# A gated cross-attention block: the first chunk's attention by tiles of tokens, layer one begun on the first tile, and three weight steps moved

## The chip, the cores and the metric

The kernel runs on one core of a Trainium2 chip. The metric is the device time of one execution in microseconds (us). Times inside the trace are counted from the first instruction.

## The reference

```
x = x + tanh(g_xattn) * Attention(layernorm(x), ctx)       # 16 heads of 32, 128 keys per batch
x = x + tanh(g_ffn)   * FFN(layernorm(x))
Attention: Q = n @ Wq + bq; K, V = ctx @ Wk + bk, ctx @ Wv + bv
           softmax(Q K^T / sqrt(32)) V, then @ Wo + bo
FFN:       h = concat(n, -n); h = s0 * h @ (+-1 by k0); relu * 2      # 1024 -> 2048
           h = s1 * h @ (+-1 by k1); relu * 2; h = s2 * h @ (+-1 by k2)   # 2048 -> 2048 -> 512
```
x has 2 x 2048 tokens of 512 features, ctx 2 x 128 keys. All inputs are float32; k0, k1, k2 are booleans in 32-bit words.

## The kernel before

The 4096 tokens are taken in sixteen chunks of 256, each of two tiles of 128. Products are in float16 pairs (a high part and what it leaves, "hi" and "lo"); the weights of the FFN are signs in 8-bit floats, built on the chip from the words of k0, k1, k2. ScalarE makes the high parts, VectorE the low ones.

Every chunk's FFN is a list of 44 slots (`SLOTS`): eight of layer one (L0, one pair of output tiles each), two that end the chunk before, then layer one to two (L1) in four groups q of seven products, with the products of layer three (L2) between. Into these slots the attention of the next chunk is woven (`WEAVE`): in slots 10 to 24 the scores S of eight units, one slot later their probabilities (PS), from slot 15 the products with V (PV), from 28 the transposition and projection of the result (CT, WO), the second norm (N2, T2), and the first norm of the chunk after that (LN, N1, T1). A unit is four heads for one tile of tokens. All five engines walk the same lists in order; semaphores join them. Chunk 0 multiplies plainly; from chunk 1 on L1 uses seven products of half-size blocks instead of eight, for which VectorE makes sums of weights: `weight_step(q, step)`, at the slots of `LATE_WEIGHTS` (first table chunk 0, second chunk 1).

The attention of chunk 0 has nothing to be woven into. It is the opening, written out by hand as the list `FIRST`: LN, N1, T1 (transposition to xT), CQ (Wq split), CX (context transposed), SCALARS, then Q (query product of one group of four heads), QP and QD (its high and low part), K, KP (key product, scaled and split), KM (the key block masked by head), V, VP, and rounds k = 0 to 9 with S, EX (exponents), PT (transposition of the probabilities, split by ScalarE and then VectorE), PV (product with V, then on VectorE reciprocal, scaling and sum into attn), with extra items of `EARLY` and `MIDDLE` in each round. CO and CL split Wo, BO and XB add the output bias to x, W0 makes the signs of layer one (one item: four of its sixteen tiles). The slots of chunk 0 follow.

A bank is one of eight in PSUM. `FIRST_BANK` gives each item of the opening a bank, and TensorE waits in `begin` for the item that had it before.

The lines of the profile: L1043 transpositions, L1066 K, L1075 V, L1103 S, L1120 to L1122 Q, L1129 and L1130 PV, L1136 to L1138 WO, L1219 and L1220 layer one, L1252 and L1253 L1. On VectorE L942 is CQ, L912 CX, L919 KP, L801 the maxima, L756 the reciprocal that begins PV, L748 PT, L763 the sum into attn, L984 to L994 the weight steps; on ScalarE L526 is EX, L570 PT, L619 a copy of a partial sum.

Of the kernel before, what the change touches and what calls it, by code (L numbers as in the profile page):

```python
# [5 lines left out]
P = 128  # L6


def gated_block_kernel(nc: bass.Bass, x, ctx, g_xattn, g_ffn, Wq, Wk, Wv, Wo, bq, bk, bv, bo,
# [118 lines left out]
    for k in range(U + 2):  # L128
# [30 lines left out]
    with es:  # L159
# [82 lines left out]
        head_zero, head_made, k_masked, k_masked_0 = (sem(n) for n in ("head_zero", "head_made", "k_masked", "k_masked_0"))  # L242
# [30 lines left out]
        CUT = {"T1": 0, "CT": TT, "T2": 2 * TT}  # L273

# [139 lines left out]
        def _(pool):  # L414
# [10 lines left out]
            def prepare(item):  # L425
# [6 lines left out]
                if kind == "KM" and n:  # L432
                    pool.wait_ge(head_made, 4)
                    pool.wait_ge(k_lo, n + 1)
                    for hl in range(2):
                        pool.tensor_tensor(
                            Kb[:, hl, n, :].rearrange("p (j k) -> p j k", j=4),
                            KHL[:, hl, n, 0:P].rearrange("p (o k) -> p o k", o=1).to_broadcast([P, 4, P]),
                            own_head[:, :].rearrange("p (j o) -> p j o", o=1).to_broadcast([P, 4, P]),
                            ALU.mult).then_inc(k_masked, 1)  # L440
# [45 lines left out]
        def _(act):  # L486
# [44 lines left out]
            def query_parts(n, a, bank):  # L531
# [9 lines left out]
                if a == 0 and n >= 2:  # L541
                    act.wait_ge(s_done, nth(0, NU, TT * (n - 2) + TT - 1))
# [785 lines left out]
```

## Time and profile before

| | |
|---|---|
| median of 3 runs | 1574.0 us (1572.46 to 1574.11) |
| the profiled execution | 1570.58 us, span 1568.8 us |
| TensorE busy | 1523.2 us, 97% |
| VectorE busy | 938.5 us, 60% |
| ScalarE busy | 672.3 us, 43% |
| granted TensorE clock, mean | 0.996 |

Busy shares are means over the whole span. TensorE bounds the chunks, the opening is a chain over several engines.

### The profile page before, as it was taken

How to read it: one execution, taken by the hardware profiler on the slowest of the kernel's cores; microseconds unless marked ns; L12 is line 12 of the kernel's file. 1: busy time of each engine (PE TensorE's matmuls, PEld its weight loads, DVE VectorE, ACT ScalarE, POOL GpSimd, SP SyncE). 2: the span in 40 equal slices, each digit the busy share in tenths (PEclk: the TensorE clock that was granted, in tenths of full speed). 3: DMA queues.
4: the chain of work that ended last, by engine and by line, in shares of the span. 5: the costliest groups of instructions: out<-in, count | busy, mean ns of one | idle time of the engine just before them, and what ended most of it. 6: DMA issues, size and time to landing. Idle time of an engine off the chain costs nothing.

```text
span 1568.8 us, 46139 instructions
## 1 busy us (share of the span) xinstructions
PE 1523.2 (97%) x19872; PEld 1300.0 (83%) x19872; DVE 938.5 (60%) x1938; ACT 672.3 (43%) x1568; POOL 169.1 (11%) x273
## 2 busy tenths in 40 slices
PE   6798999999999999999999999999999999999998
PEld 4586888888988888898988888888898888889887
DVE  5877775656556565655656566465655656565441
ACT  3442342534535254452635445253553525345231
POOL 2202001020100202001020100101010010101000
PEclk9999999999999999999999999999999999999999
DMA  8443133242424334253442524333242432314100
GB/s 255 121 103 60 42 95 69 79 79 57 87 59 99 62 81 83 52 98 56 95 69 62 95 50 102 63 88 69 62 89 52 102 66 82 82 47 98 28 29 15
DMA packets 278227, 120.96 MB, mean 77 GB/s; under 512 B 243464, under 2 KB 259848, under 8 KB 277896
## 3 DMA queue, kind: packets, MB, share of 16 engines
q1 hardware_dynamic: 275960, 117.48, 34.6%
q8 instruction: 157, 2.57, 0.7%
q10 hardware_dynamic: 2064, 0.53, 0.2%
q14 instruction: 46, 0.38, 0.1%
HBM read 37.76 MB, written 16.78 MB: 35 GB/s over the span
## 4 chain that ended last, share of the span: by engine, by line
PE 87%; DVE 6%; ACT 3%; DMA 2%; issue 2%; SPq 0%; POOL 0%; DVEq 0%; ACTq 0%; POOLq 0%
PE bank L1252 22%; PE bank L1253 22%; PE bank L1219 7%; PE bank L1220 7%; PE bank L1269 6%; PE bank L1270 6%; PE bank L1136 2%; PE bank L1137 2%; PE bank L1138 2%; PE bank L1120 2%; PE bank L1121 2%; PE bank L1122 2%; ACT Pf L526 1%; PE bank L1164 1%; DMA PT<-Phl 1%
## 5 line engine op out<-in xcount | busy, mean ns | idle before, releaser
L1252 PE MATMUL bank<-H,W 128*128 128x128 f16 x6720 | 778.3, 219 | 8.3 <-ACT C L619 6.7
L1253 PE MATMUL bank<-H,W 128*128 128x128 f16 x6720 | 778.0, 219 | 0.0
L1252 PEld LDWEIGHTS bank<-H,W 128*128 128x128 fp8e5 x6720 | 655.3, 98 | 20.8 <-ACT C L619 12.3
L1253 PEld LDWEIGHTS bank<-H,W 128*128 128x128 fp8e5 x6720 | 657.4, 98 | 7.1
L1219 PE MATMUL bank<-hT,W 128*128 128x256 f16 x1024 | 226.8, 273 | 3.5 <-DVE hT L742 1.9
L1220 PE MATMUL bank<-hT,W 128*128 128x256 f16 x1024 | 226.8, 272 | 0.0
L526 ACT ACTIVATE Pf<-bank,nmax 128x128 f32<-128x128 f32 x512 | 145.9, 368 | 139.1 <-DVE nmax L801 137.4
L1269 PE MATMUL bank<-W,h 128*128 128x512 fp8e5 x512 | 194.0, 379 | 1.6 <-DVE h L849 1.6
L1270 PE MATMUL bank<-W,h 128*128 128x512 fp8e5 x512 | 194.0, 379 | 0.0
L473 POOL TENSOR_TENSOR attn<-pvs 128x128 f32<-128x128 f32 x120 | 75.6, 630 | 1002.8 <-DVE pvs L814 1002.8
L841 DVE TENSOR_TENSOR C<-bank,C 128x256 f32<-128x256 f32 x180 | 76.2, 423 | 161.8 <-ACT C L619 89.9
L619 ACT ACTIVATE C<-bank 128x256 f32<-128x256 f32 x180 | 69.7, 387 | 212.8 <-PE bank L1253 212.8
L805 DVE SCALAR_TENSOR_TENSOR Phl<-Pf,Phl 128x512 f16<-128x512 f32 x120 | 82.5, 688 | 91.7 <-ACT Phl L604 91.6
L836 DVE TENSOR_TENSOR H<-Fp,H 128x896 f16<-128x896 f32 (+1 forms) x128 | 135.2, 1058 | 0.8 <-ACT H L610 0.8
L644 ACT ACTIVATE Fp<-bank 128x512 f32<-128x512 f32 x128 | 76.4, 597 | 90.2 <-PE bank L1220 88.9
L615 ACT ACTIVATE H<-Fp 128x896 f16<-128x896 f32 x120 | 113.3, 944 | 1.8 <-DVE Fp L872 1.7
L849 DVE SCALAR_TENSOR_TENSOR h<-C,h 128x256 f16<-128x256 f32 x180 | 76.4, 424 | 61.2 <-ACT h L682 29.6
L1219 PEld LDWEIGHTS bank<-hT,W 128*128 128x128 fp8e5 x1024 | 100.2, 98 | 15.4 <-issue 4.0
L1220 PEld LDWEIGHTS bank<-hT,W 128*128 128x128 fp8e5 x1024 | 100.2, 98 | 11.4
L801 DVE TENSOR_REDUCE nmax<-bank 128x4 f32<-128x512 f32 x128 | 87.5, 683 | 17.7 <-PE bank L1164 16.6
L1269 PEld LDWEIGHTS bank<-W,h 128*128 128x128 f16 x512 | 50.0, 98 | 53.1 <-issue 1.7
L1270 PEld LDWEIGHTS bank<-W,h 128*128 128x128 f16 x512 | 50.0, 98 | 51.3
(129 smaller groups left out, 1911.3 us busy)
## 6 DMA issues: line engine op xcount, KB each, us to landing
Qst<-q_bounce SPq DMA_DIRECT2D x120, 128.0 KB, 2.8
Y<-in_x_dram SPq DMA_DIRECT2D x16, 512.0 KB, 3.8
R<-X SPq DMA_DIRECT2D x16, 512.0 KB, 3.5
q_bounce<-Qhl SPq DMA_DIRECT2D x120, 64.0 KB
out_dram<-R SPq DMA_DIRECT2D x15, 512.0 KB, 2.7
W<-in_L_ffn_k_dram SPq DMA_DIRECT2D x8, 512.0 KB, 8.2
W<-in_L_ffn_k_dram SPq DMA_DIRECT2D x2, 1024.0 KB, 18.7
PT<-Phl SPq DMA_TRANSPOSE x120, 3.1
```

Of the source, the lines that this page charges most:

```text
L526: last = nc.scalar.activation(Pf[:, n % 2, j * P:(j + 1) * P], bank[:, j * P:(j + 1) * P], ACT.Exp, bias=nmax[:, n % 2, j:j + 1], scale=1.0)
L615: nc.scalar.activation(H0[:, 0, i], Fp[:, i % 3, 1:8, :], ACT.Copy).then_inc(l0_hi, 1)
L644: nc.scalar.activation(Fp[:, n % 3, 0:4, :], banks[n % 3][:, :].rearrange("p (b n) -> p b n", b=4), ACT.Relu)\
L801: V_.tensor_reduce(nmax[:, n % 2, :], bank[:, :].rearrange("p (j k) -> p j k", j=4), AX.X, ALU.max, negate=True).then_inc(s_max, 1)
L805: V_.scalar_tensor_tensor(out=Phl[:, n % 2, 1, :], in0=Pf[:, n % 2, :], scalar=PS, in1=Phl[:, n % 2, 0, :], op0=ALU.mult, op1=ALU.subtract)\
L836: V_.tensor_tensor(H0[:, 1, i, rows, :], Fp[:, i % 3, of, :], H0[:, 0, i, rows, :], ALU.subtract)\
L1219: mm(o, w, hT[:, k, :], start=k == 0, stop=False)
L1220: last = mm(o, w, hT[:, KT + k, :], start=False, stop=k == KT - 1)
L1252: mm(o, w, H0[:, 0, i, b_of, :], start=first, stop=False, skip_group_check=True)
L1253: last = mm(o, w, H0[:, 1, i, b_of, :], start=False, stop=i == PAIRS - 1, skip_group_check=True)
L1269: mm(banks[3 + t][:, :], hi, w2, start=q == 0 and h == 0 and jj == 0, stop=False)
L1270: last = mm(banks[3 + t][:, :], lo, w2, start=False, stop=q == GROUPS - 1 and h == 1 and jj == 1)
```

## The change

In the opening:
- A unit n of chunk 0 is now group n % 4 of tile n // 4 (`unit`), so the first tile goes through all heads first. Queries and keys of all four groups are made by round 1; groups 2 and 3 of the queries get a home of their own in Qst.
- CT for the first tile comes in round 5, WO0 in round 7, N2 and W0's first item in round 8, T2 in round 9. After the second tile's CT the first tile of pairs 0, 1 and 2 of layer one is computed (`L0T`, `layer_one(n, 0, P)`); the slots of chunk 0 then compute only the second tile of these pairs.
- `WARM`: 14 products of zeros before T1 and 6 before the scalars, into bank 1, which nobody reads.
- The context's transpositions use banks 4 and 5 instead of 6 and 7; the transposed context moves from hT to H0; keys' float copies share four places.
- The low mask of the keys moves from POOL to VectorE for groups 1 to 3; the high one stays.
- The second item of W0 moves from slot 0 of chunk 0 into the opening.

In chunk 1: the weight steps (3, 2), (3, 3), (3, 4) move from slots 15, 19, 23 to 25, 29, 33.

```diff
-    FIRST = first(("LN", 0), ("LN", 1), ("N1", 0), ("N1", 1), ("T1", 0), ("T1", 1), ("CQ", 0), ("CQ", 1), ("CQ", 2),
-                  ("CQ", 3), ("CX", 0), ("CX", 1), ("SCALARS", 0), ("Q", 0), ("Q", 1), ("QP", 0), ("QD", 0),
-                  ("K", 0), ("KP", 0), ("QP", 1), ("KM", 0), ("K", 1), ("KP", 1), ("KM", 1), ("QD", 1), ("S", 0))
-    EARLY = {1: first(("KP", 2), ("KM", 2)), 2: first(("QP", 2), ("VP", 0)), 3: first(("KP", 3), ("KM", 3)),
-             4: first(("QP", 3)), 5: first(("KP", 4)), 6: first(("KP", 5)), 7: first(("KP", 6)), 8: first(("KP", 7))}
-    MIDDLE = {0: first(("V", 0), ("K", 2)), 1: first(("V", 1), ("Q", 2)), 2: first(("QD", 2), ("K", 3)),
-              3: first(("Q", 3), ("BO", 0)), 4: first(("QD", 3), ("XB", 0), ("K", 4), ("CO", 0)),
-              5: first(("XB", 1), ("K", 5), ("CL", 0), ("CO", 1)), 6: first(("K", 6), ("CL", 1), ("CO", 2)),
-              7: first(("K", 7), ("CL", 2), ("CO", 3)), 8: first(("CL", 3)), 9: first(("W0", 0))}
+    FIRST = first(("LN", 0), ("LN", 1), ("N1", 0), ("N1", 1), ("WARM", 14), ("T1", 0), ("T1", 1), ("CQ", 0), ("CQ", 1),
+                  ("CQ", 2), ("CQ", 3), ("CX", 0), ("CX", 1), ("WARM", 6), ("SCALARS", 0), ("Q", 0), ("Q", 1),
+                  ("QP", 0), ("QD", 0), ("K", 0), ("KP", 0), ("QP", 1), ("KM", 0), ("K", 1), ("KP", 1), ("KM", 1),
+                  ("QD", 1), ("Q", 2), ("K", 2), ("S", 0))
+    EARLY = {0: first(("QP", 2), ("KP", 2), ("KM", 2), ("QD", 2)),
+             1: first(("QP", 3), ("KP", 3), ("KM", 3), ("QD", 3)), 2: first(("VP", 0)),
+             5: first(("KP", 4)), 6: first(("KP", 5)), 7: first(("KP", 6)), 8: first(("KP", 7))}
+    MIDDLE = {0: first(("Q", 3), ("K", 3), ("V", 0)), 1: first(("V", 1), ("CO", 0)), 2: first(("CO", 1), ("CL", 0)),
+              3: first(("CO", 2), ("CL", 1), ("BO", 0)), 4: first(("K", 4), ("CO", 3), ("CL", 2), ("XB", 0)),
+              5: first(("K", 5), ("CL", 3), ("XB", 1)), 6: first(("K", 6)), 7: first(("K", 7), ("WO", 0)),
+              8: first(("N2", 0), ("W0", 0)), 9: first(("T2", 0))}
...
-        FIRST += first(("CT", k - 8)) if k >= 8 else []
-    FIRST += [(1, ("LN", 0)), (1, ("LN", 1))]
-    FIRST += first(("WO", 0), ("WO", 1), ("N2", 0), ("N2", 1), ("V", 2), ("V", 3), ("T2", 0), ("T2", 1))
+        FIRST += first(("CT", 0)) if k == 5 else []
+    FIRST += first(("CT", 1), ("W0", 1), ("V", 2), ("WO", 1), ("L0T", 0), ("L0T", 1), ("V", 3)) + [(1, ("LN", 0))]
+    FIRST += first(("N2", 1)) + [(1, ("LN", 1))] + first(("T2", 1), ("L0T", 2))
...
-    FIRST_FFN = {0: ("W0", 1), 1: ("W0", 2), 3: ("W0", 3), 5: ("VP", 1)}
+    FIRST_FFN = {1: ("W0", 2), 3: ("W0", 3), 5: ("VP", 1)}
...
-                    {11: (2, 4), 15: (3, 2), 19: (3, 3), 23: (3, 4)})
+                    {11: (2, 4), 25: (3, 2), 29: (3, 3), 33: (3, 4)})
+    def unit(n, a):
+
+        return divmod(n, TT) if a else (n % G, n // G)
...
-    KIND_BANKS = {"V": (4, 4), "S": (0, 1), "PT": (2, 3), "PV": (4, 5), "T1": (2, 3), "CT": (2, 3), "WO": (0, 1)}
+    KIND_BANKS = {"CX": (4, 5), "V": (4, 4), "S": (0, 1), "PT": (2, 3), "PV": (4, 5), "T1": (2, 3), "CT": (2, 3), "WO": (0, 7)}
...
+                if kind == "WARM":
+                    pe.wait_ge(zeros_made, 1)
+                    idle = PT[:, 1].rearrange("p a n -> p (a n)")
+                    for _ in range(n):
+                        mm(banks[1][:, :], idle[:, 0:P], idle[:, 0:4 * P], start=True, stop=True)
...
+                if kind == "L0T":
+                    pe.wait_ge(w0_made, n + 2)
+                    pe.wait_ge(first_lo, FIRST_CUT["T2", 0])
+                    layer_one(n, 0, P)
...
+            def layer_one(n, begin, end):
+
+                for half in range(2):
+                    o = banks[n % 3][:, half * CHUNK + begin:half * CHUNK + end]
+                    tile = n + half * PAIRS
+                    for k in range(KT):
+                        w = W0[:, k, tile * P:(tile + 1) * P]
+                        mm(o, w, hT[:, k, begin:end], start=k == 0, stop=False)
+                        last = mm(o, w, hT[:, KT + k, begin:end], start=False, stop=k == KT - 1)
+                return last
...
+                    begun = f == 0 and ("L0T", n) in FIRST_BANK
+                    layer_one(n, P if begun else 0, CHUNK).then_inc(l0_done, 1)
```

## Rows read from the trace of the kernel before

**Rows 1.** The page, busy us by engine (share of the span, instructions).
```profile
PE 1523.2 (97%) x19872; PEld 1300.0 (83%) x19872; DVE 938.5 (60%) x1938; ACT 672.3 (43%) x1568; POOL 169.1 (11%) x273
```
**Rows 2.** Timeline of TensorE, layer one's first product in chunks 0 to 3.
```profile
74.01 0.27 PE L1219 MATMUL bank<-hT,W 128*128 128x256 f16 x1 [1.88 <-DVE hT L742]
...
177.75 0.27 PE L1219 MATMUL bank<-hT,W 128*128 128x256 f16 x1 [1.63 <-DVE h L856]
...
274.07 0.27 PE L1219 MATMUL bank<-hT,W 128*128 128x256 f16 x1
...
366.77 0.27 PE L1219 MATMUL bank<-hT,W 128*128 128x256 f16 x1
```
**Rows 3.** Waits of TensorE in 0 to 74 us: us in total, times, longest.
```profile
PE bank L1129 <- DVE PT L748: 5.8, 6, 1.5
```
**Rows 4.** Timeline of ScalarE and VectorE late in the opening's rounds.
```profile
53.02 1.12 ACT L526 ACTIVATE Pf<-bank,nmax 128x128 f32<-128x128 f32 x4
...
55.17 0.69 DVE L748 SCALAR_TENSOR_TENSOR PT<-bank,PT 128x512 f16<-128x512 f32 x1 [0.51 <-ACT PT L570]
...
59.47 0.17 DVE L756 RECIPROCAL rden<-bank 128x4 f32<-128x4 f32 x1
```
**Rows 5.** Windows: length, busy PE, PEld, DVE, ACT, POOL, granted clock, DMA share, GB/s.
```profile
15.70:19.10 3.40, 3.40 (x18) 2.36 (x17) 1.93 (x12) 1.00 (x3) 0.00 (x0) 0.50 1.05 407
...
60.00:63.40 3.40, 2.83 (x9) 1.61 (x10) 3.23 (x10) 0.60 (x1) 0.00 (x0) 0.51 0.30 79
```
**Rows 6.** Timeline of TensorE in chunk 1, the two waits in question.
```profile
221.64 0.23 PE L1252 MATMUL bank<-H,W 128*128 128x128 f16 x1 [2.34 <-ACT C L619]
...
236.47 0.22 PE L1252 MATMUL bank<-H,W 128*128 128x128 f16 x1 [0.61 <-DVE h L849]
```
**Rows 7.** Timeline of VectorE ahead of the first of them.
```profile
214.87 2.28 DVE L986 SCALAR_TENSOR_TENSOR W<-W 128x2048 fp8e5<-128x2048 fp8e5 x1
```
**Rows 8.** The chain in the opening: start, us on it; two scores, eight products.
```profile
23.04 1.75 PE bank L1103 x8
```
**Rows 9.** Timeline of the opening's first steps, all engines, and of one late step.
```profile
8.55 1.97 PE L1043 MATMUL bank<-ident,xn 128*128 128x128 f32 x8 [8.55 <-DVE xn L783]
...
11.80 2.48 DVE L942 SCALAR_TENSOR_TENSOR Wq_lo<-W,Wq_hi 128x512 f16<-128x512 f32 x4
...
14.94 0.28 PE L1120 MATMUL bank<-xT,Wq_hi 128*128 128x256 f16 x1 [2.71 <-DVE hT L912]
...
15.65 0.20 ACT L517 ACTIVATE c<-scal 128x2 f32<-128x2 f32 x1 [2.42 <-DMA scal<-in_L_ffn_s_dram]
...
20.40 0.35 DVE L919 TENSOR_SCALAR Qst<-bank,bk_c 128x128 f32<-128x128 f32 x1 [2.01 <-PE bank L1066]
...
71.10 1.04 PE L1043 MATMUL bank<-ident,xn 128*128 128x128 f32 x8
```
**Rows 10.** Timeline, POOL beside VectorE; L763 min/median/max ns; POOL's masks as a group.
```profile
46.52 1.27 POOL L443 TENSOR_TENSOR X<-Y,bo_b 128x512 f32<-128x512 f32 x1
...
46.90 1.04 DVE L763 TENSOR_TENSOR attn<-pvs 128x128 f32<-128x128 f32 x1
...
L763 DVE TENSOR_TENSOR attn<-pvs x8: 291/292/1045, 37.2 to 60.1; 128x128 f32<-128x128 f32 x8
...
L436 POOL TENSOR_TENSOR h<-Fp,own_head 128x512 f16<-128x512 f16 x6 | 6.2, 1047 | 0.4
```
**Rows 11.** Windows of VectorE alone: WO's work, then one W0 item.
```profile
65.26:67.02 1.76, 1.62 (x3) 1.00 0.19 58
78.47:80.71 2.24, 2.10 (x7) 1.00 0.61 115
```
**Rows 12.** Timeline of TensorE: the second product of 256 columns, and two of 128.
```profile
74.12 0.27 PE L1220 MATMUL bank<-hT,W 128*128 128x256 f16 x1
...
1540.95 0.22 PE L1252 MATMUL bank<-H,W 128*128 128x128 f16 x1
1541.00 0.22 PE L1253 MATMUL bank<-H,W 128*128 128x128 f16 x1
```

More of the change, by code:

```diff
@@ L273, in gated_block_kernel @@
         CUT = {"T1": 0, "CT": TT, "T2": 2 * TT}
+        FIRST_CUT = {item: n + 1 for n, item in enumerate(i for i in FIRST_ITEMS if i[0] in CUT)}
         def nth(chunk, per_chunk, n):
@@ L284, in gated_block_kernel, with query_home @@
             c[:, n:n + 1] for n in range(13))
+        def query_home(n, a):
+            return Qhl_later[:, n - 2] if a == 0 and n >= 2 else Qhl[:, n % 2]
         def wait_apart(engine, semaphore, value):
@@ L289, in wait_apart, with mask_keys @@
             engine.nop(nofuse=True)
+        def mask_keys(engine, n, hl, semaphore):
+            engine.tensor_tensor(
+                Kb[:, hl, n, :].rearrange("p (j k) -> p j k", j=4),
+                KHL[:, hl, n, 0:P].rearrange("p (o k) -> p o k", o=1).to_broadcast([P, 4, P]),
+                own_head[:, :].rearrange("p (j o) -> p j o", o=1).to_broadcast([P, 4, P]),
+                ALU.mult).then_inc(semaphore, 1)
         block = es.enter_context(nc.Block())
@@ L433, in prepare @@
                     pool.wait_ge(head_made, 4)
[L434 to L440, printed above, removed]
+                    mask_keys(pool, n, 0, k_masked_hi)
             def add_bias(a, t):
@@ L469, in attend @@
                 if kind == "PV" and a:
-                    g, t = divmod(n, TT)
+                    g, t = unit(n, a)
                     pool.wait_ge(pv_scaled, nth(a, NU, n))
@@ L540, in query_parts @@
                     act.wait_ge(s_done, nth(0, NU, TT * (n + 2) + TT - 1))
-                if a == 0 and n >= 2:
-                    act.wait_ge(s_done, nth(0, NU, TT * (n - 2) + TT - 1))
-                nc.scalar.activation(Qhl[:, n % 2, 0, :], bank[:, 0:CHUNK], ACT.Identity,
+                nc.scalar.activation(query_home(n, a)[:, 0, :], bank[:, 0:CHUNK], ACT.Identity,
                                      bias=bq_c[:, n:n + 1], scale=1 / (XS * WS))
@@ L553, in attend_first @@
                 if kind in CUT:
-                    act.wait_ge(first_turned, CUT[kind] + n + 1)
+                    act.wait_ge(first_turned, FIRST_CUT[item])
                     if kind == "CT":
@@ L751, in attend_first @@
                 if kind == "PV":
-                    g, t = divmod(n, TT)
+                    g, t = unit(n, 0)
                     v = bank.rearrange("p (j n) -> p j n", j=4)
@@ L930, in prepare @@
                         .then_inc(v_lo, 1)
-                if kind == "KM" and n == 0:
+                if kind == "KM":
                     dve.wait_ge(head_made, 4)
-                    for hl in range(2):
-                        dve.wait_ge(k_lo if hl else k_hi, 1)
-                        V_.tensor_tensor(
-                            Kb[:, hl, 0, :].rearrange("p (j k) -> p j k", j=4),
-                            KHL[:, hl, 0, 0:P].rearrange("p (o k) -> p o k", o=1).to_broadcast([P, 4, P]),
-                            own_head[:, :].rearrange("p (j o) -> p j o", o=1).to_broadcast([P, 4, P]),
-                            ALU.mult).then_inc(k_masked_0, 1)
+                    if n == 0:
+                        dve.wait_ge(k_hi, 1)
+                        mask_keys(V_, 0, 0, k_masked)
+                    dve.wait_ge(k_lo, n + 1)
+                    mask_keys(V_, n, 1, k_masked)
                 if kind == "CQ":
@@ L1001, in last_weights @@
                     .then_inc(w2_made, 1)
+            V_.memset(PT[:, 1], 0.0).then_inc(zeros_made, 1)
             V_.memset(own_head[:, :], 0.0).then_inc(head_zero, 1)
@@ L1092, in begin @@
                         pe.wait_ge(wq_lo, KT)
[L1093 removed]
+                        pe.wait_ge(first_lo, FIRST_CUT["T1", TT - 1])
                     queries(n, bank)
                 if kind == "S":
[L1096 removed]
+                    g, t = unit(n, 0)
                     pe.wait_ge(q_lo, g + 1)
[L1098 to L1101 removed]
+                    pe.wait_ge(k_masked, g + 2)
+                    if g > 0:
+                        pe.wait_ge(k_masked_hi, g)
                     for i, (hl_q, hl_k) in enumerate(((0, 0), (1, 0), (0, 1), (1, 1))):
[L1103 removed]
+                        last = mm(bank[:, :], query_home(g, 0)[:, hl_q, t * P:(t + 1) * P], Kb[:, hl_k, g, :],
                                   start=i == 0, stop=i == 3)
@@ L1123, in queries, with weighted @@
                 last.then_inc(q_done, 1)
-            def weighted(n, bank, batch):
-                g, t = divmod(n, TT)
+            def weighted(n, bank, a):
+                batch = a // PER_BATCH
+                g, t = unit(n, a)
                 for j in range(4):
@@ L1157, in attend @@
                 if kind == "S":
-                    g, t = divmod(n, TT)
+                    g, t = unit(n, a)
                     if n == 0 and a == 1:
@@ L1168, in attend @@
                     pe.wait_ge(p_crossed[n % 2], nth_sent(a, NU, n))
-                    weighted(n, bank, batch)
+                    weighted(n, bank, a)
                 if kind == "WO":
@@ L1213, in feed @@
                         pe.wait_ge(l1_sum, nth(f - 2, NC, NC - 1))
-                    for half in range(2):
-                        o = banks[n % 3][:, half * CHUNK:(half + 1) * CHUNK]
-                        for k in range(KT):
-                            tile = n + half * PAIRS
-                            w = W0[:, k, tile * P:(tile + 1) * P]
-                            mm(o, w, hT[:, k, :], start=k == 0, stop=False)
-                            last = mm(o, w, hT[:, KT + k, :], start=False, stop=k == KT - 1)
-                    last.then_inc(l0_done, 1)
+                    begun = f == 0 and ("L0T", n) in FIRST_BANK
+                    layer_one(n, P if begun else 0, CHUNK).then_inc(l0_done, 1)
                 if kind == "L1" and f == 0:
```

29 lines of the change are left out of this document (13 added, 16 removed).

## Prediction

> **What bounds the kernel now.** I read the page first: TensorE is busy 97% of the span and VectorE 60% [rows 1]. So the time is the opening before TensorE's work becomes dense, then sixteen chunks of dense products, and what is gained in between is what TensorE waits for less. The timeline of TensorE gives the frame: layer one of chunk 0 begins at 74.01, of chunk 1 at 177.75, of chunk 2 at 274.07, of chunk 3 at 366.77 [rows 2]. The third chunk took 92.70 us, the second 96.32 for the same products, 3.6 more.
>
> The timeline of the opening shows 8.6 us before the first transposition (x and its norm must come) and 2.7 before the first product for the queries [rows 9], the view of waits 5.8 in six waits for VectorE's half of the transposed probabilities (PT) [rows 3]. The opening has two parts. To some 35 us it is a line of dependent steps (queries, keys, first scores). From there to the end VectorE and ScalarE set the pace: in the last full round ScalarE's exponents start at 53.02, VectorE's PT only at 55.17, after 0.51 of waiting for ScalarE's [rows 4], and TensorE waits for the latter. Three stretches of 3.4 us ran at a granted clock of 0.50 or 0.51, that is 1.2 GHz, in the midst of it (the first and the last in [rows 5]).
>
> **The change, part by part.** It has two halves that do not touch: the new order of the opening, and three weight steps moved in chunk 1. I work each out against the profiled execution (span 1568.8, run 1570.6) and carry the difference to the median, 1574.0, which is 3.4 above that run.
>
> *Weight steps.* Steps 2, 3 and 4 for group 3 go from slots 15, 19 and 23 of chunk 1 to 25, 29 and 33. In chunk 1 TensorE waited 2.34 us at 221.64 and 0.61 at 236.47 [rows 6], 2.95 together. The first is on ScalarE's copy of a partial sum (L619), which in its order stands behind exponents, and those wait for VectorE's maxima; VectorE was late with them because the step at L986 held it for 2.28 us from 214.87 [rows 7]. Slots 15 to 24 are also those where VectorE does the maxima and the low halves for eight units. From slot 25 on no maxima are left. Slot 25 has one low half, slots 29 and 30 the end of a unit. The last step ends in slot 33 and is needed at slot 35: TensorE has slot 34's products and an output projection between. I cost the new places at nothing; if the step of slot 33 delays the second norm instead, there are ten slots to the next chunk. Bounds: 3.6 us if all that chunk 1 has over chunk 2 goes, nothing if the waits come back in the later slots. I take 2.95.
>
> *Warm products.* Fourteen zero products of 512 columns before T1 wait only for a memset; two scores' eight took 1.75 at the full clock [rows 8], so 14 take 3.1 us, 6.1 at half of it, and both end before T1's start at 8.55 [rows 9]. They cost nothing. What they can give is T1: eight transpositions took 1.97 there and 1.04 at 71.10. T1 is on the path to VectorE's split of Wq, which starts at 11.80 [rows 9] behind T1's low halves; I take 0.7 earlier. Against it: Wq must have landed, and 2.48 us of splitting follow anyway. The six before the queries fill a hole in which TensorE waits for that split.
> The Trainium skill ("TensorE: Matmul & The Clock Gate", Part 1) says that the array's default is the throttled clock and sustained activity releases it, which would favour the warm products; its Part 4 says that transpositions do not count as activity. By the last, T1 itself stays slow and the sum is 0.7 worse; the trace shows only that later transpositions are fast.
>
> *Context on banks 4 and 5.* The first query product waited until 14.94 for VectorE's copy of the context out of bank 6 [rows 9]. Now it waits for the split alone, another 0.6. With the 0.7 it starts at 13.6, and at 2.4 GHz both query groups take 2.6 us, where 4.3 were spent because of the first low stretch. But the next step, ScalarE's take of the queries, sits behind the scalars, and their tanh starts at 15.65 because of a transfer [rows 9]. So the first key comes to VectorE at 18.0 instead of 20.40: 2.4 gained.
>
> *Q2 and K2 ahead of S0, Q3 and K3 ahead of S2.* Those are the same products, done earlier. S0 comes to 22.6, against 23.0 now [rows 8]. From K1 to the first transposed probabilities TensorE then has 12.5 us of work (S at 0.87 [rows 8], Q 12 products at 0.11 [rows 2, 12]; K 0.9 and V 1.75 in the same chain) in one row, to 32.1.
>
> *The masks of heads 1 to 3.* POOL keeps the high one (1.05 us each), VectorE takes the low one. Both read SBUF and both are released by the same event, so they start together. Whether they collide the trace tells: VectorE's sum of two SBUF tensors takes 0.29, but 1.04 when POOL's bias add was under way from 46.52, and it then ended just as that did [rows 10]. So each low mask waits one POOL mask, 1.05, three times. Two of these lie beside TensorE's row of work; I leave 0.7 on the path. Bounds 0 and 3.1.
> The Trainium skill ("SBUF — State Buffer", Who interferes with whom) says that a VectorE instruction with two SBUF inputs and a GpSimd one that reads SBUF share a port, and the one that starts second blocks fully. The trace agrees in the row just named; it speaks against this part of the change.
>
> *The rounds.* I then laid the new order out engine by engine with the durations above. The eighth exponents start at 53.6, against 53.02 [rows 4]. Nothing is won by then: the rounds are lighter by the early keys and queries, but V's split now stands ahead of the third exponents, and CT0 stands before the seventh, costing 1.1.
> Behind it is the costly part. Output projection WO0 is now between PV5 and PT6 on TensorE and on VectorE. After PV5 comes K7 (0.9), then WO0 (12 products of 512 columns, as scores have them, at 1.75 / 8 [rows 8], 2.6). VectorE has nothing in that time and idles 2.6 us, then works on WO0 for 1.76 [rows 11]; then W0's first item, 2.24 [rows 11], stands ahead of the last PT. So the last PV reaches VectorE at 65.1, 5.6 later than the 59.47 of before [rows 4]. What remains is shorter by that much: WO1 alone, 68.4 to 71.0; VectorE and POOL's norm to 73.9; T21 at 74.5; its halves of hT to 76.5. Layer one of chunk 0 starts at 76.6 instead of 74.01.
> But by then three pairs have their first tile done. A product of 256 columns is issued each 0.11 us [rows 2, 12], one of 128 each 0.055 [rows 12], so the split costs nothing, and each of the three pairs has 0.88 left of 1.75. Pair 3 starts at 76.6 + 2.64 = 79.24; before it was 74.01 + 5.25 = 79.26. The opening comes out even. Bounds: 2.6 sooner with the masks uncollided and a wait less in the rounds; 5 later, below.
>
> *The rest.* The second W0 item leaves slot 0 of chunk 0; the third must be made by pair 4 at 81.0 and ends at 80.5 to 81: no wait, none to spare. On SP's queue the bounce of the keys waits for the last key, 3 to 4 us later than before; its landing is needed by layer one at 76.6 and the stacked keys by 95. Other SP items (second x, W2, k1) wait on the same events at about the same times. Nothing there.
>
> Sum: 0.0 for the opening, −2.95 for chunk 1: 1574.0 − 2.95 = 1571.0 (0.19% less).
>
> **The rivals.** A change within 0.2%, 3.1 us, can't be told from none here.
> - *Even opening, weight waits gone.* The forecast, 1571.0, own range 1569.4 to 1572.7. Chance 0.45. It sits on the bound of what can be told, so half of it counts as faster.
> - *The opening gains too.* For: three low stretches cost it some 5 us of TensorE time before (three times 3.4 at half [rows 5]), the denser row of work from 19 to 32 has none of the pauses; if the masks do not collide (0.7) and the rounds keep 2 more of the 2.4 gained at 18 us, the opening gives 3 and the time is 1568. Against: two thirds of that is beside ScalarE's and VectorE's chain. Chance 0.27.
> - *Slower: WO0 amid the rounds at 1.2 GHz.* From 43 to 65 us TensorE is now sparser than before, and the stretch at 60.00 [rows 5] shows that the clock falls there even now. WO0 is 2.6 us more at half clock, with VectorE waiting behind it; V2 and WO1 1.8 and 2.6 more. With both, the opening is 5 to 7 later and the time 1576 to 1578; it decides once more than 2.95 is lost, that is WO0 and a good part of another. Against: before, only half a projection fell into it. Chance 0.13.
> - *The weight steps only move their wait.* At slots 29 and 33 a 2.28 us step ahead of the unit's end or of the norm makes the transposes late; then 1574, no change. Against: TensorE's slot is 3.5 us and the step starts at its beginning. Chance 0.15.
>
> **How the numbers follow.** Faster by over 0.2%: 0.27, and 0.20 of the first: 0.47. Within: 0.25 of the first and 0.14 of the last: 0.39. Slower: 0.13 and 0.01: 0.14. The range takes in the second and the last and the near end of the third: 1566.5 to 1575.5.
>
> **What would show it.** In the trace after: chunk 1 at 93.0 to 93.7 us instead of 96.3; first query product near 13.6; first key on VectorE near 18; low masks of 1.8 us beside POOL; an idle 2.6 us on VectorE before WO0's add; layer one at 76 to 77, and the fourth pair near 79.2. A fourth pair by 76.5, or after 82, would make the prediction wrong, as would a wait of over 1 us in slots 25 to 35 of chunk 1. The granted clock between 50 and 70 us decides between the second and the third.

## The result, and the profile after

The changed kernel took 1578.0 us, the one before 1572.5 on the same chip (medians of 11 runs each). The ratio is 1.0037, with a 95% interval of 1.0028 to 1.0045: 5.8 us slower by the ratio (the medians differ by 5.5), where 3.0 faster had been forecast, and outside the range of 1566.5 to 1575.5. The 1574.0 that the forecast started from was the median of the first three executions of the kernel before. One of the eleven executions of the changed kernel took 5630 us; nothing here explains it, and it is left out of the ratio. The profiled execution took 1578.46, span 1576.7, which is 7.9 more than the span of before. That is 2 more than the ratio says, since the traced execution of before was a short one (1570.58, against a median of 1572.5).

The page of the changed kernel, busy time by engine. Against [rows 1] TensorE is busy 6.5 us more, with 68 more products: 20 are the products of zeros and 48 come from the split of three pairs. VectorE has 4.4 more, and POOL 4.2 less. How much of this lies on the path the page cannot say; the timeline can:

```profile
PE 1529.7 (97%) x19940; PEld 1302.1 (83%) x19940; DVE 942.9 (60%) x1942; ACT 672.8 (43%) x1568; POOL 164.9 (10%) x270
```

The timeline of TensorE after, layer one's products: the first of `L0T`, the first second-tile one (slot 0), the fourth pair, the fifth, then chunks 1, 2 and 3. Columns are start, duration, operands, and in brackets the idle time before with what ended it:

```profile
77.54 0.22 PE L1147 MATMUL bank<-hT,W 128*128 128x128 f16 x1
83.42 0.22 PE L1147 MATMUL bank<-hT,W 128*128 128x128 f16 x1 [0.76 <-DVE hT L756]
86.10 0.27 PE L1147 MATMUL bank<-hT,W 128*128 128x256 f16 x1
89.31 0.28 PE L1147 MATMUL bank<-hT,W 128*128 128x256 f16 x1 [1.31 <-DVE W L983]
187.12 0.27 PE L1147 MATMUL bank<-hT,W 128*128 128x256 f16 x1 [1.63 <-DVE h L870]
281.62 0.27 PE L1147 MATMUL bank<-hT,W 128*128 128x256 f16 x1
374.28 0.27 PE L1147 MATMUL bank<-hT,W 128*128 128x256 f16 x1
```

Read against [rows 2], this is where the time went. The fourth pair starts at 86.10; before it started at 74.01 + 5.25 = 79.26. That is 6.8 later. The fifth waits 1.31 for its signs and is 8.3 late (it started at 81.00 before). The rest of chunk 0 costs another 1.1 (187.12 against 177.75 is 9.4); in it TensorE waits 1.38 for xT, which it did not before, and 1.24 instead of 0.59 for the stacked queries. Chunk 1 then took 94.50 instead of 96.32 and gave 1.8 back; from chunk 2 on nothing moves (92.66 here, 92.70 before).

So the loss is in the opening. Its steps after, from the timelines of ScalarE, VectorE and POOL; they answer to [rows 4, 9, 10]:

```profile
16.59 0.20 ACT L533 ACTIVATE c<-scal 128x2 f32<-128x2 f32 x1 [4.14 <-DMA scal<-in_L_ffn_s_dram]
18.85 0.35 DVE L935 TENSOR_SCALAR Qst<-bank,bk_c 128x128 f32<-128x128 f32 x1
23.59 1.04 POOL L307 TENSOR_TENSOR h<-Fp,own_head 128x512 f16<-128x512 f16 x1
23.73 1.44 DVE L307 TENSOR_TENSOR h<-Fp,own_head 128x512 f16<-128x512 f16 x1 [0.95 <-POOL Fp L452]
56.62 1.12 ACT L542 ACTIVATE Pf<-bank,nmax 128x128 f32<-128x128 f32 x4
61.95 0.75 DVE L835 SCALAR_TENSOR_TENSOR X<-bank,c,X 128x512 f32<-128x512 f32 x1 [4.28 <-PE bank L1173]
69.94 0.18 DVE L770 RECIPROCAL rden<-bank 128x4 f32<-128x4 f32 x1 [0.78 <-PE bank L1165]
```

The eighth exponents start at 56.62 where the forecast had 53.6: 3.0 late. VectorE then idles 4.28 before WO0's add where it had 2.6: 1.7 more. The last PV reaches VectorE at 69.94, forecast 65.1: 4.8 late. Second-tile layer one starts at 83.42, forecast 76.6: 6.8 late.

The windows of the changed kernel show where TensorE was slow. Columns: stretch, length, busy time and count of PE, PEld, DVE, ACT, POOL, then the granted clock, DMA share, GB/s:

```profile
20.30:23.70 3.40, 3.38 (x17) 2.97 (x18) 1.25 (x3) 0.31 (x1) 0.49 (x2) 0.55 1.05 386
43.30:46.70 3.40, 3.40 (x22) 2.90 (x23) 1.92 (x5) 0.50 (x1) 0.57 (x1) 0.57 0.00 0
57.40:60.80 3.40, 3.40 (x11) 1.28 (x10) 0.27 (x1) 0.35 (x2) 0.00 (x0) 0.51 0.90 197
69.30:72.70 3.40, 3.15 (x18) 2.69 (x19) 1.65 (x4) 1.21 (x2) 0.00 (x0) 0.50 0.29 85
```

In four stretches the mean granted clock is 0.50 to 0.57, that is, TensorE ran at 1.2 GHz for all or nearly all of them: K1 and the start of Q2; K4, a transposition and scores; the first two thirds of WO0 (VectorE is busy 0.27 of 3.40); the transpositions of the second tile's result and V2. Of V2 the timeline says it plainly; at the full clock, in experiment 2, it took 1.89:

```profile
71.93 3.18 PE L1095 MATMUL bank<-W,H 128*128 128x256 f32 x8
```

### The profile page after: what moved, and what is told of

The parts are those of the page before. It is cut to its first block, busy times and chain, and to the rows that moved or that the text cites. A ratio compares the mean times of both kernels' runs of the same rounds, so it can differ in the third digit from the quotient of the medians.

```text
span 1576.7 us, 46288 instructions
## 1 busy us (share of the span) xinstructions
PE 1529.7 (97%) x19940; PEld 1302.1 (83%) x19940; DVE 942.9 (60%) x1942; ACT 672.8 (43%) x1568; POOL 164.9 (10%) x270
## 4 chain that ended last, share of the span: by engine, by line
PE 85%; DVE 7%; ACT 4%; issue 2%; DMA 2%; ACTq 0%; POOL 0%; SPq 0%; DVEq 0%; POOLq 0%
PE bank L1281 21%; PE bank L1282 21%; PE bank L1298 7%; PE bank L1299 7%; PE bank L1147 7%; PE bank L1148 7%; PE bank L1171 2%; PE bank L1172 2%; PE bank L1173 2%; ACT Pf L542 2%; PE bank L1154 2%; PE bank L1155 2%; PE bank L1156 2%; PE bank L1199 1%; DVE nmax L815 1%
## 5 line engine op out<-in xcount | busy, mean ns | idle before, releaser
L1281 PEld LDWEIGHTS bank<-H,W 128*128 128x128 fp8e5 x6720 | 655.3, 98 | 17.9 <-ACT C L633 10.1
L1147 PE MATMUL bank<-hT,W 128*128 128x256 f16 (+1 forms) x1048 | 227.2, 270 | 3.7 <-DVE h L870 1.6
L1148 PE MATMUL bank<-hT,W 128*128 128x256 f16 (+1 forms) x1048 | 227.3, 270 | 0.0
L1147 PEld LDWEIGHTS bank<-hT,W 128*128 128x128 fp8e5 x1048 | 102.5, 98 | 15.6 <-issue 2.8
L1148 PEld LDWEIGHTS bank<-hT,W 128*128 128x128 fp8e5 x1048 | 102.6, 98 | 11.3
```

The source lines that it names most:

```text
L1147: mm(o, w, hT[:, k, begin:end], start=k == 0, stop=False)
L1148: last = mm(o, w, hT[:, KT + k, begin:end], start=False, stop=k == KT - 1)
L1281: mm(o, w, H0[:, 0, i, b_of, :], start=first, stop=False, skip_group_check=True)
```

## The experiments

Theory A, after reading the trace: the loss is the clock, which falls in the sparser rounds, with WO0's two engines in line behind each other. Theory B: the new order itself costs the time (VectorE idle in WO0, W0 ahead of the last PT, masks beside POOL), at any clock. Ratios are to the kernel before, timed beside each run.

Where traces are compared one caution holds. Kernels with the same code in the opening did not have the same opening in time: layer one began at 74.01 in the trace of before and at 75.75 in that of e1, at 71.75 in that of e6 and at 70.19 in that of e12. So a single time in the opening is good to some 1.7 us, and a smaller difference between two traces shows nothing by itself.

**1. The parts alone, in the old order.** Only the table of weight steps (e1); only the warm products (14, and 6 ahead of the scalars) and the context's banks (e2); both (e5).

```diff
# e1_weights_only
-                    {11: (2, 4), 15: (3, 2), 19: (3, 3), 23: (3, 4)})
+                    {11: (2, 4), 25: (3, 2), 29: (3, 3), 33: (3, 4)})
# e2_early_only
-    FIRST = first(("LN", 0), ("LN", 1), ("N1", 0), ("N1", 1), ("T1", 0), ("T1", 1), ("CQ", 0), ("CQ", 1), ("CQ", 2),
+    FIRST = first(("LN", 0), ("LN", 1), ("N1", 0), ("N1", 1), ("WARM", 14), ("T1", 0), ("T1", 1), ("CQ", 0), ("CQ", 1), ("CQ", 2),
...
-    KIND_BANKS = {"V": (4, 4), "S": (0, 1), "PT": (2, 3), "PV": (4, 5), "T1": (2, 3), "CT": (2, 3), "WO": (0, 1)}
+    KIND_BANKS = {"CX": (4, 5), "V": (4, 4), "S": (0, 1), "PT": (2, 3), "PV": (4, 5), "T1": (2, 3), "CT": (2, 3), "WO": (0, 1)}
```

> The kernel before with only the three weight steps moved. Theory (the two halves are independent, the opening alone made the change slow): the opening is as before, chunk 1 takes 94.5 us instead of 96.3 as it did in the changed kernel, and the time is 1.8 to 2.9 us less than before. Rival (the weight steps' new slots cost something further on, in chunk 1 or 2): the time is as before or above it, and a new wait for a transposed probability or for the norm is seen at slots 29 to 35.

> The kernel before with only the products of zeros (14 and 6) and the context on banks 4 and 5. Theory (the early part is sound and its gain is lost later): first query product at 13.7, first key on VectorE 1.5 to 2.4 us sooner than 20.40, and some of that, 0.5 to 1.5 us, reaches layer one; the time is 0 to 1.5 us less than before. Rival (the early part itself costs, by moving the low-clock stretch from the queries to a costlier place): layer one begins later than 74.0.

> The kernel before with the early part (14 and 6 unused products, context on banks 4 and 5) and the moved weight steps, without the new order. Theory (the two gains are in different places and add): ratio near 0.9984 times 0.9989, 0.9973, 4 us less than before. Rival (the early gain was noise of the clock's phase): 0.9984 as with the weights alone.

Measured: weights alone 0.9984 (0.9975 to 0.9992), 2.5 us; early part alone 0.9989 (0.9980 to 0.9998), 1.7 us; both 0.9973 (0.9963 to 0.9983), 4.2 us. The two add up. Layer one of chunk 0 started at 72.40 with the early part (before 74.01); this 1.6 alone would be within the spread of traces, the ratio is what shows the gain.

With the weight steps alone chunk 1 took 94.01 instead of 96.32, and these waits of TensorE are left in it (columns: total, times, longest):

```profile
PE bank L1219 <- DVE h L856: 1.6, 1, 1.6
PE bank L1252 <- ACT C L619: 0.6, 1, 0.6
PE bank L1129 <- DMA PT<-Phl: 0.5, 1, 0.5
```

The 2.34 of [rows 6] is gone. The last line is for the transposed probabilities. In the changed kernel it is 0.99, and VectorE's timeline shows the step of slot 25 ahead of the low half of the last unit:

```profile
244.16 2.28 DVE L1000 SCALAR_TENSOR_TENSOR W<-W 128x2048 fp8e5<-128x2048 fp8e5 x1
246.91 0.68 DVE L819 SCALAR_TENSOR_TENSOR Phl<-Pf,Phl 128x512 f16<-128x512 f32 x1
```

The table is not the whole cause of that wait, since e2, which has the old table, shows 0.8 of it, and before shows none.

What follows: the changed kernel is these two parts and the new order (with the masks and `L0T` in it). 1.0037 / 0.9973 is 1.0064, so the new order costs some 10 us, nearly twice the loss that the ratio shows. By the two intervals together the 10 is good to about 2.

**2. The clock held.** The changed kernel with 45 more products of 512 columns, in places where TensorE waited; they write to banks that nobody reads at the time. Nothing of the order changes.

```diff
+    HOLD = {0: (4, 1, 0), 1: (6, 1, 0), 2: (8, 7, 4), 3: (6, 7, 6), 4: (7, 6, 7), 5: (14, 6, 7)}
+    for n, kind, m in ((0, "K", 0), (1, "K", 1), (2, "PV", 2), (3, "PV", 5), (4, "PV", 6), (5, "PV", 7)):
+        FIRST.insert(FIRST.index((0, (kind, m))), (0, ("HOLD", n)))
...
+                if kind == "HOLD":
+                    count, to, keys = HOLD[n]
+                    if keys:
+                        pe.wait_ge(k_float, keys)
+                    for _ in range(count):
+                        mm(banks[to][:, :], Wq_hi[:, 0, 0:P], Wq_hi[:, 0, 0:4 * P], start=True, stop=True)
```

> The changed kernel with 45 more unused products of 512 columns in six holes of TensorE: before K0, K1, PV2, PV5, PV6 and PV7. They read the high part of Wq and write banks that are free there. Theory A (the opening is slow because the clock falls to 1.2 GHz in K1, in round 4, in WO0 and in T2, V2): these stretches vanish, WO0 takes 2.6 us instead of 4.3 and V2 1.9 instead of 3.2, the fourth pair of layer one starts 4 to 6 us earlier, the time is 4 to 6 us less than the changed kernel's, at or below that of before. Rival B (the order makes it slow: WO0 and W0 stand ahead of the last PT on VectorE): at most 1.5 us of it comes back.

Measured: 1.0010 (1.0001 to 1.0019), so 0.9973 of the changed kernel, 4.2 us less, with the two intervals apart. The same four windows of this kernel:

```profile
20.30:23.70 3.40, 3.40 (x31) 2.87 (x29) 2.13 (x4) 0.78 (x2) 1.42 (x2) 1.00 1.07 391
43.30:46.70 3.40, 2.76 (x26) 1.90 (x23) 2.87 (x7) 1.94 (x6) 1.21 (x2) 1.00 0.02 5
57.40:60.80 3.40, 2.82 (x25) 1.74 (x24) 2.73 (x7) 0.91 (x2) 0.95 (x3) 1.00 0.61 118
69.30:72.70 3.40, 3.40 (x36) 2.33 (x35) 2.54 (x6) 0.00 (x0) 0.00 (x0) 1.00 0.35 95
```

And its timeline at five of the forecast's steps, with V2 among them:

```profile
53.92 1.12 ACT L545 ACTIVATE Pf<-bank,nmax 128x128 f32<-128x128 f32 x4
57.57 0.75 DVE L838 SCALAR_TENSOR_TENSOR X<-bank,c,X 128x512 f32<-128x512 f32 x1 [2.60 <-PE bank L1182]
65.36 0.18 DVE L773 RECIPROCAL rden<-bank 128x4 f32<-128x4 f32 x1 [0.59 <-PE bank L1174]
66.93 1.89 PE L1104 MATMUL bank<-W,H 128*128 128x256 f32 x8
79.80 0.27 PE L1156 MATMUL bank<-hT,W 128*128 128x256 f16 x1
83.02 0.28 PE L1156 MATMUL bank<-hT,W 128*128 128x256 f16 x1 [1.30 <-DVE W L986]
```

Forecast were 53.6, an idle 2.6, 65.1 and 79.24. With the clock at its full level the schedule worked out holds to 0.6 us; of the 6.8 that the fourth pair was late, 6.3 went. So theory A holds for the opening. Not all of the 6.3 is the clock: in this trace the scalars' transfer also came 0.9 sooner, which brought the first key forward by 0.5 (18.36 against 18.85). And the trace is of this kernel's shortest execution (1571.39, median 1573.11), so what the clock costs in time is better read from the ratio, 4.2. But the time stays 0.1% above before, not below it, so B holds too, for the rest: the fifth pair's wait of 1.30 does not depend on the clock, and see 4.

**3. WO0 later.** The changed kernel with W0's first item and WO0 behind the last PT instead of between PV5 and PT6.

```diff
-              5: first(("K", 5), ("CL", 3), ("XB", 1)), 6: first(("K", 6)), 7: first(("K", 7), ("WO", 0)),
-              8: first(("N2", 0), ("W0", 0)), 9: first(("T2", 0))}
+              5: first(("K", 5), ("CL", 3), ("XB", 1)), 6: first(("K", 6)), 7: first(("K", 7))}
+    at = FIRST.index((0, ("PV", 7)))
+    FIRST[at:at + 1] = first(("W0", 0), ("WO", 0), ("PV", 7), ("N2", 0), ("T2", 0))
```

> The changed kernel with WO0, N2 and the first W0 item behind the last PT (order PT7, W0, WO0, PV7, N2, T2) and nothing else. Theory A (clock): WO0 is still at 1.2 GHz or the next stretch is; 0 to 2 us come back. Rival B (order): VectorE no longer idles for WO0 and the last PT does not wait for 2.24 us of W0, so the last PV reaches VectorE 3 to 4 us sooner and 3 to 5 us come back.

Measured: 1.0025 (1.0015 to 1.0035), 1.9 us less than the changed kernel, but the intervals overlap. That is what theory A expected (0 to 2) and less than B's 3 to 5. The fourth pair starts at 85.15 instead of 86.10, in the trace of the longest of nine executions. WO0 now ran at the full clock (its products take 0.38 each), but TensorE stood at 0.50 to 0.54 from 40.0 to 50.2, and again over V2 and the start of WO1:

```profile
85.15 0.27 PE L1148 MATMUL bank<-hT,W 128*128 128x256 f16 x1
71.70:75.10 3.40, 3.40 (x11) 1.87 (x11) 2.83 (x8) 0.00 (x0) 0.00 (x0) 0.60 0.52 128
```

**4. The order, with the clock held in both.** The old order with 27 products that hold the clock (e6), on top of the two parts of experiment 1; and the new order with experiments 2 and 3 together (e7).

```diff
# e6_early_weights_hold: e5 and, by the same "HOLD" item (the first of them waits for q_split)
+    HOLD = {0: (5, 7, 3), 1: (3, 6, 5), 2: (5, 7, 6), 3: (5, 6, 7), 4: (2, 6, 7), 5: (2, 6, 7), 6: (5, 6, 7)}
+    for n, kind, m in ((0, "PV", 0), (1, "PV", 4), (2, "PV", 5), (3, "PV", 6), (4, "CT", 0), (5, "PV", 7), (6, "CT", 1)):
# e7_hold_later: e3 and e4, with
+    HOLD = {0: (4, 1, 0), 1: (6, 1, 0), 2: (8, 7, 4), 3: (6, 7, 6), 4: (6, 6, 7), 5: (12, 6, 7)}
```

> The kernel before with the early part, the moved weight steps and 27 more unused products in seven holes of the old order (before PV0, PV4 to PV7, CT0, CT1). Theory (the two stretches at 1.2 GHz that the old order has left, at some 36 and 60 us, cost it 2 to 3 us): another 1 to 3 us less than with the early part and weights alone, layer one 1 to 3 us sooner, no window of the opening below a clock of 0.9. Rival (those stretches lie beside VectorE's and ScalarE's chain): no difference.

> The changed kernel with the unused products in its holes and also WO0, N2 and the first W0 item behind the last PT. Theory (with the clock held, what is left of the loss is the order: VectorE idle for WO0 and the last PT behind W0): 2 to 3 us less than with the holes filled alone, so 1 to 3 us less than before. Rival (the order is innocent, as the same move brought little without the held clock): within 1 us of the kernel with filled holes alone.

Measured: e6 0.9961 (0.9948 to 0.9975), median 1566.45 of five executions; e7 0.9996 (0.9988 to 1.0005).

e7 is e4 with such products added and nothing else, so it is experiment 2 over again: from 1.0025 to 0.9996, 4.5 us less, with the intervals apart. So two pairs of kernels show the clock's price in the new order. Against e3, e7 is 2.2 us less, as the theory said (2 to 3), but the intervals overlap and its trace does not have the fourth pair sooner (80.13 against 79.80): that WO0's place costs 2 us is likely and not shown.

Between 58 and 61.5 us, the windows of e5 (first) and e6 (second) differ in the clock:

```profile
58.00:61.50 3.50, 3.50 (x11) 1.79 (x12) 3.36 (x9) 0.60 (x1) 0.00 (x0) 0.50 0.28 79
```
```profile
58.00:61.50 3.50, 3.18 (x24) 1.64 (x24) 3.27 (x10) 0.60 (x1) 0.00 (x0) 1.00 0.81 178
```

yet VectorE is as busy in the one as in the other (3.36, 3.27). In the old order VectorE sets the pace there, so a slow TensorE should cost little. e6 against e5 is 0.9988, 1.9 us, good to about 2.6: that fits, but it shuts out neither nothing nor a price as in the other. In the new order one of the slow stretches lies where VectorE waits (0.27 busy), and the clock is worth 4.2 and 4.5.

The order still loses 0.0035 between e6 and e7, some 5.5 us. The fourth pair comes at 80.13 in e7, and at 71.75 + 5.25 = 77.00 in e6, which is 3.1 of it, and the fifth pair's wait is another 1.3. The remaining 1 us wasn't traced.

```profile
80.13 0.27 PE L1157 MATMUL bank<-hT,W 128*128 128x256 f16 x1
```
```profile
71.75 0.27 PE L1235 MATMUL bank<-hT,W 128*128 128x256 f16 x1 [1.88 <-DVE hT L746]
```

One stretch of e7 (37.5 to 41, granted 0.54) and of e6 (20.5 to 23.9, 0.60) stayed slow. The pair e3 and e9 (see 8) has no slow stretch in the opening on either side, and shows the same: e9's fourth pair is at 69.91 + 5.25 = 75.16, 4.6 ahead of e3's, and its ratio 0.9968 against 1.0010 is 6.6 us less. The four traces of the new order with such products have the fourth pair at 78.56 to 80.67 (e8, e3, e7, e10), the three of the old order at 75.16 to 77.00 (e9, e12, e6).

**5. The third W0 item sooner.** e7 with W0's item in slot 0 instead of slot 1 of chunk 0.

```diff
-    FIRST_FFN = {1: ("W0", 2), 3: ("W0", 3), 5: ("VP", 1)}
+    FIRST_FFN = {0: ("W0", 2), 3: ("W0", 3), 5: ("VP", 1)}
```

> As the previous one, with the third W0 item at slot 0 of chunk 0 instead of slot 1, ahead of the first norm. Theory (the fourth pair's successor waits 1.3 us for that item because the norm and T1 stand ahead of it): that wait goes, and if the norm's transfer to xT is not late for the queries in slot 4, the time is 0.5 to 1.3 us less than the previous one's. Rival (the queries then wait for the transfer instead): no difference, with a wait of about 1 us at the first query product.

Measured: 1.0012 (1.0003 to 1.0021), 2.5 us more than e7, with the intervals just touching: no gain, and probably a loss. TensorE's waits from 78 to 180 have no line for W0 any more, and these two ahead of the rest:

```profile
PE bank L1174 <- DMA PT<-Phl: 3.4, 2, 2.7
PE bank L1164 <- DMA xT<-xs: 2.5, 1, 2.5
```

In e7 the first line is the same 3.4, the second is the 1.3 for W0, and there is none for xT. L1164 is the first query product, where the rival put the new wait, but at 1 us. So the wait moved to another place and grew; which of VectorE's steps passed it on wasn't traced.

**6. The masks.** e3 with both masks of groups 1 to 3 on POOL.

> The changed kernel with its holes filled, and both masks of groups 1 to 3 on POOL again. Theory (each low mask on VectorE takes 1.44 us beside POOL's against 0.78 alone, so the split brings little): within 1 us of the kernel with filled holes, either way; the first probabilities' split starts within 0.7 us of 32.8. Rival (the masks on two engines are what lets the scores come early): 1.5 to 3 us more.

Measured: 1.0001 (0.9992 to 1.0010) against e3's 1.0010; the split of the first probabilities starts at 32.71, as expected (32.8). POOL's two masks in a row:

```profile
22.50 2.04 POOL L310 TENSOR_TENSOR h<-Fp,own_head 128x512 f16<-128x512 f16 x2
```

In the changed kernel the same masks, by tile and engine (columns: count, then duration min/median/max in ns, first and last start):

```profile
L307 DVE TENSOR_TENSOR h<-Fp,own_head x5: 679/1443/1443, 19.6 to 31.5; 128x512 f16<-128x512 f16 x5
L307 POOL TENSOR_TENSOR h<-Fp,own_head x3: 1038/1039/1041, 23.6 to 31.4; 128x512 f16<-128x512 f16 x3
```

VectorE's two for group 0, with POOL still, took 1.55 together; the three beside POOL's took 1.44 each. So a pair is ready 1.6 us after its start when split (23.59 to 25.17), 2.04 on POOL alone, and VectorE pays 1.44 for the 0.46 gained. By the ratios the split brings nothing that shows; the intervals overlap.

**7. Without the first tile ahead (`L0T`).** e3 with layer one of the first three pairs whole, in slots 0 to 2.

```diff
-    FIRST += first(("CT", 1), ("W0", 1), ("V", 2), ("WO", 1), ("L0T", 0), ("L0T", 1), ("V", 3)) + [(1, ("LN", 0))]
-    FIRST += first(("N2", 1)) + [(1, ("LN", 1))] + first(("T2", 1), ("L0T", 2))
+    FIRST += first(("CT", 1), ("W0", 1), ("V", 2), ("WO", 1), ("V", 3)) + [(1, ("LN", 0))]
+    FIRST += first(("N2", 1)) + [(1, ("LN", 1))] + first(("T2", 1))
```

> The changed kernel with its holes filled, without the early first tiles of layer one. Theory (they lie in the hole in which TensorE waits for the second tile's norm, and save 3 times 0.88 us): the fourth pair starts 1.3 to 2.6 us later, and since 1.3 us of that is waited for the W0 item anyway, the time is 1.3 to 2.6 us more. Rival (they are hidden anyway or delay V3 and T2): no difference.

Measured: 1.0027 (1.0017 to 1.0037), 2.7 us more than e3, good to about 2. That is near three times 0.88, as the forecast priced it, but it does not confirm the price. Two things are mixed in it: the wait of 1.3 for the third W0 item is gone, and the clock fell at the start of layer one, after waits of 1.70 and 1.66. TensorE is busy for all of this stretch, so it cost some 1.7 (an estimate: half of 3.50). What `L0T` is worth at the full clock is therefore open:

```profile
78.50:82.00 3.50, 3.50 (x20) 2.49 (x18) 0.50 (x2) 0.38 (x1) 0.00 (x0) 0.51 0.16 62
```

**8. Two tries for a better version,** both on e6: ten more products ahead of K0 and K1 (e9), and weight steps at 27, 30 and 33 instead of 25, 29 and 33 (e12).

> The fastest kernel so far (old order, early part, moved weight steps, seven holes filled) with ten more unused products, four before K0 and six before K1, where it still had a window at a clock of 0.60. Theory (a low stretch costs where TensorE itself is on the chain, as it is from K1 to the first PT): no window below 0.9, layer one up to 1.5 us sooner, 0.5 to 1.5 us less. Rival (the phase of the clock already varies from run to run so that it costs nothing in the median): no difference.

> The old order with the early part and seven filled holes, and the weight steps of chunk 1 at slots 27, 30, 33 instead of 25, 29, 33. Theory (the step at slot 25 holds VectorE 2.28 us before the low half of the last unit's probabilities, so its transposed form comes late and TensorE waits 0.5 to 2.1 us for it in chunk 1): that wait is gone, chunk 1 takes 93.5 to 94.0 us, the time is 0.5 to 1.5 us below the same kernel with slots 25, 29, 33. Rival (the wait is of the transfer itself, not of the step ahead of it): the wait stays.

Measured: e9 0.9968 (0.9957 to 0.9980), e12 0.9963 (0.9949 to 0.9976): neither can be told from e6, and e6 and e12 rest on five executions each. In e9 layer one began at 69.91, 1.8 sooner than in e6, with no slow stretch in the opening, and chunk 1 lost it again: it took 97.37, against 94.47 in e6. A wait for the transposed probabilities came first, then a slower clock:

```profile
69.91 0.27 PE L1235 MATMUL bank<-hT,W 128*128 128x256 f16 x1 [1.88 <-DVE hT L746]
239.32 0.19 PE L1145 MATMUL bank<-V,PT 128*128 128x65 f16 x1 [2.10 <-DMA PT<-Phl]
240.00:250.00 10.00, 10.00 (x74) 6.09 (x71) 3.65 (x8) 1.32 (x3) 2.22 (x4) 0.83 0.35 86
```

In e12 the wait for the transposed probabilities is gone, but chunk 1 took 95.04 and not the 93.5 to 94.0 that was expected: a wait of 1.4 for xT stands in it instead.

## Why the prediction was wrong, and where it was right

**The step that failed** is the opening's sum, "The opening comes out even". Every term was taken "with the durations above", nearly all from rows at the full clock. The clock was in the rows [rows 5] and was made a rival of its own (0.13) instead of a term. In the sum WO0 stood with 2.6 us of idle VectorE, and it was 4.28; the eighth exponents were 3.0 late before it, and V2 took 3.18 instead of 1.89 after it. The changed kernel is in the main that rival, which named WO0 at half clock with VectorE behind it, and V2. Experiment 2 shows it: with the clock held the fourth pair comes at 79.80, forecast 79.24. The rival was not right in all: it had WO1 slow too, which ran at the full clock (75 to 77.3), and did not have the stretches at K1 and at K4. And that the median of 1578.0 lies in its 1576 to 1578 is in part luck: these times start from 1574.0, so they stand for 2 to 4 us more than before, and 5.8 was measured against 1572.5.

The clock is not the whole of the failed step. Some 10 us of loss are in the new order, and holding the clock gives back 4.2 to 4.5. The rest is the order itself at any clock, of which the third W0 item is 1.3 and the later fourth pair 3 to 4.6; why the fourth pair is later than in the old order was not taken apart further.

The prediction's argument against this rival was the weak point: "before, only half a projection fell into it" counts what fell into the slow stretch in the old order. Two things should have weighed more. The new order empties the rounds of keys and queries: from 40 to 60 us TensorE has 124 products in the trace of before and 100 in that of after, as these windows show (before first, clock 1.00; after, 0.85).

```profile
40.00:60.00 20.00, 12.71 (x124) 9.40 (x121) 16.79 (x37) 12.01 (x33) 5.03 (x7) 1.00 0.53 133
```
```profile
40.00:60.00 20.00, 14.13 (x100) 9.63 (x99) 13.66 (x32) 8.45 (x26) 3.77 (x5) 0.85 0.40 110
```

And a slow stretch costs by who waits for it: VectorE is busy 0.27 of 3.40 in WO0's, 3.36 of 3.50 in the old order's (e5). The second could be seen before: in [rows 5] VectorE is busy 3.23 of the 3.40 at 60.00, so half the clock should have cost little there.

**The denser row of work from 19 to 32** did not save the clock either: it fell at 20.3, ahead of most of that row, after TensorE had waited twice for ScalarE's queries, 1.11 and 1.58. Part of this start is a transfer that is no part of the change: the tanh came at 16.59 instead of 15.65 (in experiment 2, which has the same code up to there, at 15.68). The first key came at 18.85, forecast 18.0, and at 18.36 in experiment 2, so the transfer accounts for some 0.5 of the 0.9.

**Mis-sized:** the third W0 item, "no wait, none to spare". TensorE waits 1.3 for it at either clock (after, e3, e4, e7, e10), and experiment 5 only moved that. The item ends later than the forecast had it, where VectorE is full (busy 3.86 of 4.00 from 80 to 84 in experiment 2). Also, even with the fourth pair on time the new order is behind by the traces: the old order did not stay at 79.26 but comes to 75.2 to 77.0 with the same early parts and clock. "Even" was measured against a kernel whose own opening had 2 to 4 us to give.

**The weight steps:** forecast 2.95; measured 2.5 alone (1.3 to 3.9 by its interval, so the forecast lies in it), 2.3 by its trace and 1.8 by the changed kernel's. Chunk 1 was forecast at 93.0 to 93.7 and took 94.01 and 94.50. The mechanism was right: the 2.34 at the partial sum is gone. A part came back, as the fourth rival feared, but at slot 25, not at 29 or 33: the step stands ahead of the last unit's low half, and TensorE waits 0.5 (e1) to 2.10 (e9) for it. With the step at slot 27 (e12) chunk 1 has no such wait. Since e2 has 0.8 of it with the old table, the step's share is not known.

**Right:** the first query at 13.6 (13.68), T1 sooner (eight transpositions 1.11 instead of 1.97), and that the weight steps and the early part do not touch (their gains add). The low masks collide, as it said: 1.44 beside POOL's, against 0.78 each in the pair of group 0. The forecast had 1.8, by letting the mask wait POOL's out; that would have ended at 24.63 + 0.78 = 25.41, and it ended at 25.17.

Of the two rules of the Trainium skill ("TensorE: Matmul & The Clock Gate") that the prediction weighed, Part 1's agrees: after the warm products T1 ran in 1.11. Part 4 of that page of the Trainium skill says that the full clock does not engage for transpositions. Here T1 ran at the faster pace all the same, and the measurement decides; whether transpositions by themselves would bring it about, no run here shows.

## What to carry to other kernels

Price a new order at both clocks: mark each stretch in which TensorE gets sparser, and ask which engine waits for the work in it; where one does, the halved pace goes on the path; where that engine is busy anyway it should cost less, which these runs allow but do not show. Unused products in waits (27 and 45 here) held the clock in most of the opening. In time no price of them showed; in one trace (e12) the six before the queries ran at a mean clock of 0.57, took 2.60, and the first query started at 14.09 instead of 13.68. They are worth trying before a reordering: e6 keeps the old order and took 1566.45 us, 0.39% less than before and 0.76% less than the changed one. e9 and e12, which also keep it, can't be told from it.

## What the runs showed of the hardware that wasn't expected

- The clock fell after waits of TensorE of only 2.21 and 1.83 us; only ahead of the fourth slow stretch was one of 3.99. These rows of its timeline in the changed kernel are the first products after its waits ahead of the second and the third slow stretch (43.3 and 57.4), and T1's eight transpositions:

```profile
43.27 0.19 PE L1164 MATMUL bank<-V,PT 128*128 128x65 f16 x1 [2.21 <-DVE PT L762]
56.26 0.19 PE L1164 MATMUL bank<-V,PT 128*128 128x65 f16 x1 [1.83 <-DVE PT L762]
8.61 1.11 PE L1058 MATMUL bank<-ident,xn 128*128 128x128 f32 x8 [1.60 <-DVE xn L797]
```

- The granted clock reads 1.00 in T1's stretch before and after, though the same eight took 1.97 [rows 9] and 1.11 here. That early, the pace of the products tells more than the granted clock.
- The stretches with a low clock are not in the same places in two kernels with the same opening: in e6 one lies from 20.5 to 23.9 (0.60) and none at 10 to 13.5, in e12 it is the other way round (0.57 from 10.1 to 13.5).
- One wait of 2.10 in the midst of dense chunk 1 was followed by a mean clock of 0.83 over 10 us (e9).
